# A convolution and whitening kernel: the first eight units' filters by a matmul of their own, and the store of all filters moved back in the queue

## The chip, the cores and the metric

The kernel runs on one core of a Trainium2 chip. The metric is the device time of one execution in microseconds (us), smaller is better; a kernel's time is the median of several runs.

## The reference

There are two layers. Layer 0 is a long convolution of each of 64 channels of x (4 images of 64 channels, 256 x 256) with a filter that is an outer product of two vectors of 256, which a small network makes from positions. Layer 1 whitens the result over the 64 channels. Cut to what matters:

```python
def _implicit_filter(z, w1, b1, w2, b2, w3, b3, wo, freq, t, deltas):
    h = jnp.sin(freq * (z @ w1 + b1))
    h = jnp.sin(freq * (h @ w2 + b2))
    h = jnp.sin(freq * (h @ w3 + b3))
    h = h @ wo
    decay = jnp.exp(-t * jnp.abs(deltas))
    return h * decay
...
k = jnp.einsum('ijk,imk->ijmk', hx, hy)[0]          # a rank-1 filter per channel
...                                                  # y = causal 2-D convolution of x with k, by FFT
out = y + x * bias[:, None, None]
...
x1_s = x1[:, ::STRIDE ** 2]                          # every 9th sample of each channel
mean1 = jnp.mean(x1_s, axis=-1, keepdims=True)
cov = x1_s @ x1_s.T / x1_s.shape[1] + EPS * jnp.eye(B, dtype=x.dtype)
deconv = _isqrt_newton_schulz(cov, N_ITER)
out = deconv @ (x1 - mean1)
```

## The kernel before

**Work.** A unit is one channel of two images, 128 units in all: 64 channels in a first sweep, the same 64 in a second. Since the filter is an outer product, a unit is two multiplications by Toeplitz matrices, one from the X filter (`make_v`, f = 0) and one from the Y filter (`make_y`, f = 1). TensorE does `make_v(q + 1)` and then `make_y(q)`, each of 16 matmuls (L731 to L734). Operands are split into a rounded part and a rest (hi and lo).

**Filters.** At the start TensorE, VectorE and ScalarE run the small network in three layers (L720, L553 to L556, L487). ScalarE's Exp (L484) makes the decay. VectorE multiplies the last product with it into `filt` (L561): 128 partitions, X filters of 64 channels and then Y filters. A Toeplitz matrix needs a filter shifted by one for each row. The filters are therefore stored to DRAM in 16 duplicates, and a load (a "hankel" load, L286 and L290) reads 64 rows of 320 values, each row one value later, from the 16 duplicates. ScalarE copies each half within SBUF to get the other 64 rows (`fill`, L453; L493 for unit 0), and writes the reversed matrices (`flip`, L462 and L463; L495 and L496 for unit 0). VectorE makes the lo part (`split_t`, L582; L605 for unit 0).

**Two stores.** The store of all filters (L328, four DMAs of 768 KB, 3.15 MB) is long. So a short one comes first: for the first AHEAD = 5 units, 5 rows in 16 duplicates for X from SyncE's queue and the same for Y from ScalarE's (`store_filters`, L249). The units 0 to 4 load from that (`first_dram`), the others from `g_dram`.

**Order.** Every engine's order is written by hand, with semaphores. SyncE issues all transfers but one, in one queue:

```python
store_filters(sp, 0)
for q in range(AHEAD):
    if q == H_SLOTS:
        load_x(AHEAD - 1)
    load_hankel(q)
for k in range(0, COPIES, COPIES // 4):
    sp.dma_start(copies_of(g_dram, k, ...), filt...).then_inc(filt_stored, 16)
for q in range(UNITS):
    if q > 0:
        load_x(q + 4)
    store_y(q - 1)
    if q == 0:
        sp.wait_ge(filt_stored, 16 * 4)
    load_hankel(q + 5)
    load_kept(q)
```

There are 5 slots for x, 3 for hankel loads and 3 for the reversed matrices, so `load_hankel(q)` waits until unit q - 3 has been flipped and split. Per unit ScalarE does `round_v(q)` (L479, L481), `round_x(q + 2)` (L472), `flip(q + 2)`, `fill(q + 3)`; VectorE does `split_v(q)` (L573), `finish_y(q - 1)` (L593, which writes y and waits for the store of the y before it in the same of two buffers), `split_t(q + 2)`, `sum_masked(q - 2)` (L601); POOL does `split_x(q + 2)` (L393) and `mask_y(q - 1)` (L428). Between the last layer and unit 0 TensorE runs 15 matmuls on zeros (`warm_up(15)`, L708), which are not used.

After the last unit come the covariance, the Newton-Schulz steps and 64 tiles of the whitened output. That part is not touched.

Of the kernel before, what the change touches and what calls it, by code (L numbers as in the profile page):

```python
# [6 lines left out]
F32 = mybir.dt.float32  # L7
F32R = mybir.dt.float32r
I32 = mybir.dt.int32
ALU = mybir.AluOpType  # L10
# [20 lines left out]
AHEAD = 5  # L31
# [37 lines left out]
def conv_whiten(nc, x, first, hidden, columns, bias, out):  # L69
    g_dram = nc.dram_tensor("filters", [COPIES, COPY_PITCH], F32, kind="Internal").ap()  # L70
    first_dram = nc.dram_tensor("first_filters", [COPIES, COPY_PITCH], F32, kind="Internal").ap()
    y_dram = nc.dram_tensor("convolved", [SWEEPS * P, ROWS * XW], F32, kind="Internal").ap()

    with ExitStack() as ctx:
# [57 lines left out]
        chan_i, chan, rate = sb("chan_i", [P, 1], I32), sb("chan", [P, 1]), sb("rate", [P, 1])  # L132


        arg, near_int, hid, pos_f, pos, decay = (kept[:, k * S:(k + 1) * S] for k in range(6))
        rest = kept[:, 14 * S + MASK_COLS:15 * S + MASK_COLS]
# [46 lines left out]
        first_stored = [sem(f"first_stored{f}") for f in range(2)]  # L183
# [72 lines left out]
        def _(sp):  # L256
# [16 lines left out]
            def load_hankel(q):  # L273
# [5 lines left out]
                wait(sp, t_lo_done, q - H_SLOTS + 1)  # L279
                for f in range(2):  # L280
                    at = (f * C + q % C) * GLEN
                    spread = [[COPY_PITCH + HALF // COPIES, COPIES], [1, HALF // COPIES], [1, HW]]
# [6 lines left out]
                    src = bass.AP(tensor=g_dram.tensor, offset=at, ap=spread)  # L289
                    sp.dma_start(h_own[k][f], src).then_inc(hankel_loaded[k], 16)  # L290
# [29 lines left out]


            store_filters(sp, 0)
            for q in range(AHEAD):
                if q == H_SLOTS:
                    load_x(AHEAD - 1)
                load_hankel(q)
            for k in range(0, COPIES, COPIES // 4):
                sp.dma_start(copies_of(g_dram, k, COPIES // 4, 0, 2 * C),  # L328
                             filt.unsqueeze(1).to_broadcast([P, COPIES // 4, GLEN])).then_inc(filt_stored, 16)
            for q in range(UNITS):  # L330
# [3 lines left out]
                if q == 0:  # L334
                    sp.wait_ge(filt_stored, 16 * 4)
# [42 lines left out]
        def _(pool):  # L378
# [8 lines left out]
            def split_x(q):  # L387
                if q >= UNITS:
# [6 lines left out]

            nc.gpsimd.memset(idle, 0.0).then_inc(idle_ready, 1)
            nc.gpsimd.memset(w_sb, 0.0).then_inc(w_zeroed, 1)
            nc.gpsimd.iota(pos_i, pattern=[[-1, S]], base=S - 1, channel_multiplier=0)
            chained(nc.gpsimd.iota(chan_i[:], pattern=[[0, 1]], base=0, channel_multiplier=1))
            nc.gpsimd.tensor_copy(pos, pos_i)  # L400
            nc.gpsimd.tensor_copy(chan[:], chan_i[:]).then_inc(pos_ready, 1)
            nc.gpsimd.memset(filt, 0.0).then_inc(filt_zeroed, 1)
            nc.gpsimd.memset(small[:], 0.0).then_inc(filt_zeroed, 1)
# [40 lines left out]
        def _(act):  # L444
# [10 lines left out]
            def flip(q):  # L455
# [3 lines left out]
                act.wait_ge(h_filled, 2 * (q + 1))  # L459
# [24 lines left out]
            nc.scalar.activation(decay, pos, ACT.Exp, scale=rate[:]).then_inc(decay_ready, 1)  # L484
# [3 lines left out]
            store_filters(act, 1)  # L488
# [398 lines left out]
```

## Time and profile before

| | |
|---|---|
| median of 3 runs | 920.75 us (919.14 to 922.94) |
| profiled execution | 922.17 us, of which the traced span is 920.4 us |
| busy in the span | PE 867.4, DVE 576.6, ACT 516.5, POOL 494.5 us |
| first matmul of unit 0 | 22.37 us |
| mean granted clock of TensorE | 0.99 of full speed |

Read it as follows: the span is the traced part of one execution; the time around it is 1.8 us. An engine's busy time says how near it is to be the bound, and the views by time say where it waits.

### The profile page before, as it was taken

What the parts mean: (1) busy time and instruction counts of PE and PEld (TensorE: products, weight loads), DVE (VectorE), ACT (ScalarE), POOL (GpSimd) and SP (SyncE); (2) the same over time, 40 slices, a digit from 0 to 9 for tenths busy, and PEclk for the clock granted to TensorE, in tenths of its full rate; (3) what the DMA queues carried; (4) which work ended last, traced back from release to release, by engine and by line L of the source; (5) the groups of instructions that cost most, each with busy time, mean ns of one, the idle gap of its engine ahead of it and who ended that gap; (6) DMA issues with size and microseconds to landing.
All of it is one profiled execution on the core that took longest, in us unless ns stands there. A gap on an engine that the chain in (4) does not pass through costs nothing.

```text
span 920.4 us, 16281 instructions
## 1 busy us (share of the span) xinstructions
PE 867.4 (94%) x6252; PEld 729.0 (79%) x6252; DVE 576.6 (63%) x630; ACT 516.5 (56%) x974; POOL 494.5 (54%) x279
## 2 busy tenths in 40 slices
PE   7989999999999999999999999998999999877773
PEld 5989999999999999999999999998544444323221
DVE  3488888878888867888888888885333333322221
ACT  3667777777777756777777777771233332222120
POOL 1488888888888876777777777772000000000000
PEclk9999999999999999999999999999999999999997
DMA  3788888888888885999999999987999999999998
GB/s 127 251 266 260 264 265 262 264 266 264 263 264 264 266 262 187 335 316 321 315 328 322 326 315 327 312 284 275 413 394 427 427 427 427 427 426 427 427 427 360
DMA packets 80899, 294.07 MB, mean 320 GB/s; under 512 B 11253, under 2 KB 29878, under 8 KB 66230
## 3 DMA queue, kind: packets, MB, share of 16 engines
q1 hardware_dynamic: 80737, 292.90, 88.5%
q8 instruction: 50, 0.82, 0.3%
q14 instruction: 27, 0.22, 0.1%
q10 hardware_dynamic: 85, 0.12, 0.0%
HBM read 155.37 MB, written 137.61 MB: 318 GB/s over the span
## 4 chain that ended last, share of the span: by engine, by line
PE 81%; DMA 13%; DVE 2%; SPq 1%; ACT 1%; issue 1%; POOL 0%; DVEq 0%; ACTq 0%; POOLq 0%
PE ps L734 24%; PE ps L853 15%; PE ps L731 13%; PE ps L732 13%; PE ps L733 13%; DMA arena<-convolved 11%; PE ps L773 2%; DMA filters<-arena 1%; DMA first_filters<-arena 1%; SPq L344 1%; PE ps L793 0%; PE ps L708 0%; DVE arena L699 0%; SPq L328 0%; PE ps L720 0%
## 5 line engine op out<-in xcount | busy, mean ns | idle before, releaser
L734 PE MATMUL ps<-arena 128*128 128x128 f32 x2048 | 394.2, 274 | 0.0
L731 PE MATMUL ps<-rounded 128*128 128x256 f32 x1024 | 374.0, 365 | 7.0 <-DVE rounded L605 3.0
L428 POOL TENSOR_TENSOR arena<-arena,mask 128x1024 f32<-128x1024 f32 x126 | 325.6, 2584 | 82.0 <-DVE arena L593 81.9
L734 PEld LDWEIGHTS ps<-arena 128*128 128x128 f32 x2048 | 316.6, 190 | 0.0
L733 PE MATMUL ps<-rounded 128*128 128x256 f32 x1024 | 289.1, 282 | 0.0
L732 PE MATMUL ps<-rounded 128*128 128x256 f32 x1024 | 288.4, 282 | 0.0
L853 PE MATMUL ps<-arena 128*128 128x512 f32 x488 | 216.0, 597 | 26.6 <-DMA arena<-convolved 26.5
L593 DVE SCALAR_TENSOR_TENSOR arena<-arena,bias_sb,ps 128x1024 f32<-128x1024 f32 x127 | 162.6, 1280 | 78.4 <-PE ps L734 75.1
L853 PEld LDWEIGHTS ps<-arena 128*128 128x128 f32 x488 | 90.7, 190 | 150.9 <-issue 105.0
L731 PEld LDWEIGHTS ps<-rounded 128*128 128x128 f32 x1024 | 196.9, 192 | 8.0 <-issue 6.6
L732 PEld LDWEIGHTS ps<-rounded 128*128 128x128 f32 x1024 | 197.5, 193 | 0.0
L733 PEld LDWEIGHTS ps<-rounded 128*128 128x128 f32 x1024 | 193.2, 189 | 0.0
L393 POOL TENSOR_TENSOR rounded<-arena,rounded 128x512 fp32r<-128x512 f32 x128 | 164.6, 1286 | 52.8 <-ACT rounded L472 52.8
L699 DVE TENSOR_SCALAR arena<-ps,small 128x1024 f32<-128x1024 f32 x64 | 82.1, 1283 | 171.6 <-PE ps L853 171.6
L525 ACT ACTIVATE arena<-ps,small 128x1024 f32<-128x1024 f32 x64 | 71.3, 1114 | 189.7 <-PE ps L853 189.7
L601 DVE TENSOR_REDUCE arena<-arena 128x116 f32<-128x1044 f32 x126 | 155.5, 1234 | 0.0
L573 DVE TENSOR_TENSOR rounded<-ps,rounded 128x512 fp32r<-128x512 f32 x128 | 88.5, 692 | 46.5 <-ACT rounded L481 46.5
L479 ACT COPY arena<-ps 128x512 f32<-128x512 f32 x128 | 75.0, 586 | 72.5 <-PE ps L734 72.5
L453 ACT COPY arena<-arena 64x256 f32<-64x256 f32 x254 | 102.9, 405 | 12.3 <-DMA arena<-filters 6.1
L462 ACT COPY arena<-arena 128x256 f32<-128x256 f32 x127 | 51.5, 405 | 77.9 <-PE ps L734 77.9
L582 DVE TENSOR_TENSOR rounded<-arena,rounded 128x512 fp32r<-128x512 f32 x127 | 88.4, 696 | 2.8 <-ACT rounded L463 2.8
L472 ACT CAST rounded<-arena 128x512 fp32r<-128x512 f32 x128 | 79.5, 621 | 6.2 <-DVE arena L561 1.9
(100 smaller groups left out, 295.4 us busy)
## 6 DMA issues: line engine op xcount, KB each, us to landing
arena<-x SPq DMA_DIRECT2D x128, 512.0 KB, 4.7
convolved<-arena SPq DMA_DIRECT2D x128, 512.0 KB, 5.7
out<-arena SPq DMA_DIRECT2D x64, 1024.0 KB, 13.4
arena<-convolved SPq DMA_DIRECT2D x47, 1024.0 KB, 18.6
arena<-filters SPq DMA_DIRECT2D x246, 80.0 KB, 4.4
arena<-convolved SPq DMA_DIRECT2D x28, 512.0 KB, 5.6
filters<-arena SPq DMA_DIRECT2D x4, 768.0 KB, 6.2
rounded<-convolved SPq DMA_DIRECT2D x3, 1024.0 KB, 8.9
```

Of the source, the lines that this page charges most:

```text
L393: nc.gpsimd.tensor_tensor(x_lo[k], row_block(q % X_SLOTS, 0), x_hi[k].bitcast(F32), ALU.subtract).then_inc(x_lo_done, 1)
L428: nc.gpsimd.tensor_tensor(masked_of(k, 0, PER), by_image(y_sb[k]), mask_of(q // C, 0, PER), ALU.mult).then_inc(masked_done, 1)
L453: nc.scalar.copy(h_copied[h][f], h_source[h][f]).then_inc(h_filled, 1)
L573: nc.vector.tensor_tensor(v_lo[k], ps_v[k][:, :, 0:S], v_hi[k].bitcast(F32), ALU.subtract).then_inc(v_lo_done, 1)
L582: nc.vector.tensor_tensor(t_lo[k], hankel[h][:, :, ::-1], t_hi[k].bitcast(F32), ALU.subtract).then_inc(t_lo_done, 1)
L593: nc.vector.scalar_tensor_tensor(y_sb[k], x_sb[q % X_SLOTS], bias_sb[:, q % C:q % C + 1], ps_y[k].rearrange("p a n -> p (a n)"), ALU.mult, ...
L601: nc.vector.tensor_reduce(z_of(q % C), grouped(q % 2, 0, BLOCKS), AX_X, ALU.add).then_inc(z_done, 1)
L731: mm(wide, hi[:, b, cols], t_hi[k][:, f, :], start=True, stop=False)
L732: mm(wide, hi[:, b, cols], t_lo[k][:, f, :], start=False, stop=False)
L733: mm(wide, lo[:, b, cols], t_hi[k][:, f, :], start=False, stop=False)
L734: last = mm(o[:, b, m * S + P:(m + 1) * S], block1[:, b, cols], t_f32[k][:, f, :], start=False, stop=True)
L853: last = mm(ps[:, bank(t, u) + r, :], dmat, places[k][:, w:w + IMG], start=True, stop=True)
```

## The change

Six things are changed together.

1. The first units are now eight (AHEAD = 8). POOL makes a weight matrix `first_w` in which the last layer's column of each of eight channels, X and Y, stands eight times: 2 x 8 x 8 = 128 columns. One more matmul in the last layer (L741) puts each filter in eight partitions, VectorE multiplies it with its own decay (L575), and one DMA of 128 rows (L327), each partition to a row of its own, stores them. ScalarE's store is gone. The factor 1/(2S) on the X filters, which was an instruction of its own (L547), becomes `share`, a factor per partition in the last multiply.
2. The loads for units 0 to 7 read from these eight duplicates. For unit 0 they read all 128 rows, and the two half copies (L493) and their waits are gone.
3. In SyncE's queue unit 3's load comes before x(4), two quarters of the store of all filters come next, then unit 4's load, then the other two quarters; `load_hankel(5)` is issued without a wait for that store. Unit 8's load is the first with the wait `filt_stored`.
4. On ScalarE `fill(q + 2)` stands ahead of `round_x(q + 2)` and `flip(q + 2)`; before, it was one unit earlier, at the end of the step.
5. The channel numbers for the decay are made first on POOL, with a semaphore `chan_ready`, and VectorE computes two decay rates from them with more, small operations.
6. ScalarE computes two Exp instead of one and waits for `pos_ready` ahead of them.

The diff, cut:

```diff
-AHEAD = 5
+AHEAD, FIRST_COPIES = 8, 8
+FIRST_PITCH = 4096 + 128
...
-        def store_filters(eng, f):
-            eng.wait_ge(filt_ready, 1)
-            eng.dma_start(copies_of(first_dram, 0, COPIES, f * C, AHEAD),
-                          filt[f * C:f * C + AHEAD, :].unsqueeze(1).to_broadcast([AHEAD, COPIES, GLEN])
-                          ).then_inc(first_stored[f], 16)
...
+                if q == AHEAD:
+                    sp.wait_ge(filt_stored, 16 * 4)
                 for f in range(2):
                     if q < AHEAD:
-                        sp.wait_ge(first_stored[f], 16)
-                        src = bass.AP(tensor=first_dram.tensor, offset=at, ap=spread)
-                        sp.dma_start(h_own[k][f], src
+                        rows, cols = (HALF, HW) if q else (P, S)
+                        n = FIRST_COPIES
+                        src = bass.AP(tensor=first_dram.tensor, offset=(f * AHEAD + q) * n * FIRST_PITCH,
+                                      ap=[[FIRST_PITCH + rows // n, n], [1, rows // n], [1, cols]])
+                        sp.dma_start(h_own[k][f] if q else hankel[0][:, f, :], src
...
-            store_filters(sp, 0)
-            for q in range(AHEAD):
-                if q == H_SLOTS:
-                    load_x(AHEAD - 1)
+            sp.wait_ge(first_made, 1)
+            sp.dma_start(first_dram[:, 0:GLEN], first_filt).then_inc(first_stored, 16)
+            sp.wait_ge(first_stored, 16)
+            for q in range(H_SLOTS + 1):
                 load_hankel(q)
+            load_x(4)
+            sp.wait_ge(filt_ready, 1)
             for k in range(0, COPIES, COPIES // 4):
                 sp.dma_start(copies_of(g_dram, k, COPIES // 4, 0, 2 * C),
                              filt.unsqueeze(1).to_broadcast([P, COPIES // 4, GLEN])).then_inc(filt_stored, 16)
+                if k == COPIES // 4:
+                    load_hankel(4)
             for q in range(UNITS):
                 if q > 0:
                     load_x(q + 4)
                 store_y(q - 1)
-                if q == 0:
-                    sp.wait_ge(filt_stored, 16 * 4)
                 load_hankel(q + 5)
...
+            pool.wait_ge(hidden_loaded, 16 * 2)
+            of_first = w_sb[:, 2, :].rearrange("p (f c) -> p f c", f=2)[:, :, 0:AHEAD].unsqueeze(3)
+            nc.gpsimd.tensor_copy(first_w.rearrange("p (f c k) -> p f c k", f=2, c=AHEAD),
+                                  of_first.to_broadcast([P, 2, AHEAD, FIRST_COPIES])).then_inc(first_w_ready, 1)
...
             act.wait_ge(rate_ready, 1)
-            nc.scalar.activation(decay, pos, ACT.Exp, scale=rate[:]).then_inc(decay_ready, 1)
+            act.wait_ge(pos_ready, 1)
+            nc.scalar.activation(first_decay, pos, ACT.Exp, scale=rate[:, 1:2]).then_inc(decay_ready, 1)
+            nc.scalar.activation(decay, pos, ACT.Exp, scale=rate[:, 0:1]).then_inc(decay_ready, 1)
...
-            store_filters(act, 1)
...
-                nc.scalar.copy(h_copied[0][f], h_source[0][f]).then_inc(h_filled, 1)
-                act.wait_ge(h_filled, f + 1)
...
-            fill(2)
             for q in range(UNITS):
                 round_v(q)
+                fill(q + 2)
                 round_x(q + 2)
                 flip(q + 2)
-                fill(q + 3)
...
-            nc.vector.tensor_tensor(filt[:, 0:S], ps[:, 0, 0:S], decay, ALU.mult).then_inc(filt_ready, 1)
+            nc.vector.scalar_tensor_tensor(first_filt[:, 0:S], ps[:, 1, 0:S], share[:], first_decay, ALU.mult, ALU.mult
+                                           ).then_inc(first_made, 1)
+            dve.wait_ge(f_mm, 5)
+            nc.vector.scalar_tensor_tensor(filt[:, 0:S], ps[:, 0, 0:S], share[:], decay, ALU.mult, ALU.mult
+                                           ).then_inc(filt_ready, 1)
...
+                if layer == 2:
+                    pe.wait_ge(first_w_ready, 1)
+                    mm(ps[:, 1, 0:S], first_w, hid, start=True, stop=True).then_inc(f_mm, 1)
```

SyncE's queue from the first filters' store on, before (`first_filters` is `first_dram`, `filters` is `g_dram`, `arena` holds the slots in SBUF, `convolved` receives y):

```order
L286 DMA arena<-first_filters 64x1x320 [waits first_stored0]
L286 DMA arena<-first_filters 64x1x320 [waits first_stored1]
L271 DMA arena<-x 128x1024
L286 DMA arena<-first_filters 64x1x320 [waits first_stored0,t_lo_done,flipped]
L286 DMA arena<-first_filters 64x1x320 [waits first_stored1]
L286 DMA arena<-first_filters 64x1x320 [waits first_stored0,t_lo_done,flipped]
L286 DMA arena<-first_filters 64x1x320 [waits first_stored1]
L328 DMA filters<-arena 128x4x384 x4
L290 DMA arena<-filters 64x1x320 [waits t_lo_done,flipped,filt_stored]
L290 DMA arena<-filters 64x1x320
L271 DMA arena<-x 128x1024 [waits y_done]
```

and after, from the same place:

```order
L289 DMA arena<-first_filters 64x1x320 x4
L289 DMA arena<-first_filters 64x1x320 [waits t_lo_done,flipped]
L289 DMA arena<-first_filters 64x1x320
L271 DMA arena<-x 128x1024
L334 DMA filters<-arena 128x4x384 [waits filt_ready]
L334 DMA filters<-arena 128x4x384
L289 DMA arena<-first_filters 64x1x320 [waits t_lo_done,flipped]
L289 DMA arena<-first_filters 64x1x320
L334 DMA filters<-arena 128x4x384 x2
L289 DMA arena<-first_filters 64x1x320 [waits t_lo_done,flipped]
L289 DMA arena<-first_filters 64x1x320
L271 DMA arena<-x 128x1024 [waits y_done]
```

Unit 3's loads, with their waits for unit 0's flip and split, now stand ahead of x(4), the pair for unit 4 stands inside the store, and the pair for unit 5, behind it, no longer waits for `filt_stored`.

ScalarE's step for unit 1, before (L479 and L481 are `round_v`, L472 `round_x`, L462 and L463 `flip`, L453 `fill`):

```order
L479 COPY arena<-ps 128x512 [waits v_mm]
L481 CAST rounded<-ps 128x512
L472 CAST rounded<-arena 128x512 [waits v_mm,x_loaded3]
L462 COPY arena<-arena 128x256 [waits y_mm,h_filled]
L463 CAST rounded<-arena 128x512
L453 COPY arena<-arena 64x256 [waits hankel_loaded1]
L453 COPY arena<-arena 64x256
L479 COPY arena<-ps 128x512 [waits y_mm,v_mm]
```

and after (L489 and L491, L482, L472 and L473, L463 in the same order):

```order
L489 COPY arena<-ps 128x512 [waits v_mm]
L491 CAST rounded<-ps 128x512
L463 COPY arena<-arena 64x256 [waits hankel_loaded0]
L463 COPY arena<-arena 64x256
L482 CAST rounded<-arena 128x512 [waits v_mm,x_loaded3]
L472 COPY arena<-arena 128x256 [waits y_mm,h_filled]
L473 CAST rounded<-arena 128x512
```

The two copies of `fill`, then for unit 4 and now for unit 3, have moved from behind the flip to directly behind `round_v`.

ScalarE's first rows, before:

```order
L484 ACT_TABLE_LOAD
L484 ACTIVATE arena<-arena,rate 128x256 [waits rate_ready]
L487 ACT_TABLE_LOAD
L487 ACTIVATE arena<-arena 128x256 [waits f_dve] x3
```

and after:

```order
L495 ACT_TABLE_LOAD [waits pos_ready]
L495 ACTIVATE arena<-arena,rate 128x256 [waits rate_ready]
L496 ACTIVATE arena<-arena,rate 128x256
L499 ACT_TABLE_LOAD
L499 ACTIVATE arena<-arena 128x256 [waits f_dve] x3
```

The load of the first activation table, which stood ahead of every wait, now carries the wait for `pos_ready`.

## Rows read from the trace of the kernel before

**Rows 1.** The page, part 1: busy us (share of the span) and instructions.

```profile
PE 867.4 (94%) x6252; PEld 729.0 (79%) x6252; DVE 576.6 (63%) x630; ACT 516.5 (56%) x974; POOL 494.5 (54%) x279
```

**Rows 2.** Busy time by stretch: stretch and length, engines, PEclk, DMA share, GB/s.

```profile
49.40:53.00 3.60, 3.60 (x18) 3.60 (x19) 3.60 (x4) 2.35 (x6) 3.60 (x3) 0.53 0.90 270
60.00:70.00 10.00, 10.00 (x89) 10.00 (x87) 7.63 (x9) 7.09 (x15) 8.78 (x6) 1.00 0.86 274
```

**Rows 3.** Timeline of ScalarE: start, length, line, operation [idle before <-releaser].

```profile
20.93 0.40 ACT L493 COPY arena<-arena 64x256 f32<-64x256 f32 x1 [6.30 <-DMA arena<-first_filters]
...
23.05 0.83 ACT L453 COPY arena<-arena 64x256 f32<-64x256 f32 x2
...
24.73 0.61 ACT L463 CAST rounded<-arena 128x512 fp32r<-128x512 f32 x1
...
41.56 0.83 ACT L453 COPY arena<-arena 64x256 f32<-64x256 f32 x2 [4.43 <-DMA arena<-filters]
...
67.41 0.59 ACT L479 COPY arena<-ps 128x512 f32<-128x512 f32 x1 [0.48 <-PE ps L734]
...
72.05 0.59 ACT L479 COPY arena<-ps 128x512 f32<-128x512 f32 x1 [0.48 <-PE ps L734]
```

**Rows 4.** Timeline, rows of TensorE: the starts after a stop, and the warm-up.

```profile
12.68 6.64 PE L708 MATMUL ps<-arena 128*128 128x256 f32 x30
...
22.37 0.55 PE L731 MATMUL ps<-rounded 128*128 128x256 f32 x1 [3.05 <-DVE rounded L605]
...
26.65 0.36 PE L731 MATMUL ps<-rounded 128*128 128x256 f32 x1 [0.27 <-DVE rounded L582]
...
44.14 0.39 PE L731 MATMUL ps<-rounded 128*128 128x256 f32 x1 [1.10 <-DVE rounded L573]
...
49.34 0.45 PE L731 MATMUL ps<-rounded 128*128 128x256 f32 x1 [2.62 <-issue]
```

**Rows 5.** Waits of SyncE's own queue, 0 to 60 us: total, times, longest.

```profile
SPq L290 <- DMA filters<-arena: 6.1, 1, 6.1
```

**Rows 6.** Timeline of SyncE's queue: issue and time to issue.

```profile
13.44 0.30 SPq L249 DMA_DIRECT2D first_filters<-arena  x1
18.64 3.75 SPq L286 DMA_DIRECT2D arena<-first_filters  x6
...
27.77 4.72 SPq L328 DMA_DIRECT2D filters<-arena  x4
38.64 1.16 SPq L290 DMA_DIRECT2D arena<-filters  x2
```

**Rows 7.** Timeline of VectorE: split_t while POOL splits, and alone.

```profile
25.38 1.13 DVE L582 TENSOR_TENSOR rounded<-arena,rounded 128x512 fp32r<-128x512 f32 x1 [2.10 <-ACT rounded L463]
...
66.39 0.69 DVE L582 TENSOR_TENSOR rounded<-arena,rounded 128x512 fp32r<-128x512 f32 x1
```

**Rows 8.** Timeline of ScalarE before the filters.

```profile
0.73 1.28 ACT L484 ACT_TABLE_LOAD   x1 [0.73 <-PEq L878]
...
3.06 0.51 ACT L484 ACTIVATE arena<-arena,rate 128x256 f32<-128x256 f32 x1 [1.05 <-DVE rate L543]
...
5.80 0.42 ACT L487 ACTIVATE arena<-arena 128x256 f32<-128x256 f32 x1 [0.93 <-DVE arena L556]
```

**Rows 9.** Timeline of POOL: positions, and split_x and mask_y of a steady unit.

```profile
1.94 0.40 POOL L400 CAST arena<-arena 128x256 f32<-128x256 int32 x1
...
69.28 1.30 POOL L393 TENSOR_TENSOR rounded<-arena,rounded 128x512 fp32r<-128x512 f32 x1
71.19 2.78 POOL L428 TENSOR_TENSOR arena<-arena,mask 128x1024 f32<-128x1024 f32 x1 [0.61 <-DVE arena L593]
```

**Rows 10.** Busy time by stretch: DMA share and GB/s at the end.

```profile
14.50:15.00 0.50, 0.50 (x4) 0.45 (x3) 0.47 (x2) 0.13 (x1) 0.29 (x1) 1.00 0.31 55
20.00:20.60 0.60, 0.00 (x0) 0.00 (x0) 0.00 (x0) 0.00 (x0) 0.00 (x0) 1.00 0.49 130
29.00:37.00 8.00, 8.00 (x72) 8.00 (x72) 5.17 (x6) 6.62 (x14) 5.83 (x4) 1.00 1.01 362
```

More of the change, by code:

```diff
@@ L70, in conv_whiten @@
     g_dram = nc.dram_tensor("filters", [COPIES, COPY_PITCH], F32, kind="Internal").ap()
-    first_dram = nc.dram_tensor("first_filters", [COPIES, COPY_PITCH], F32, kind="Internal").ap()
+    first_dram = nc.dram_tensor("first_filters", [P, FIRST_PITCH], F32, kind="Internal").ap()
     y_dram = nc.dram_tensor("convolved", [SWEEPS * P, ROWS * XW], F32, kind="Internal").ap()
@@ L131, in conv_whiten @@
         col = sb("col", [P, 5])
-        chan_i, chan, rate = sb("chan_i", [P, 1], I32), sb("chan", [P, 1]), sb("rate", [P, 1])
+        chan_i, chan, rate = sb("chan_i", [P, 2], I32), sb("chan", [P, 2]), sb("rate", [P, 2])
+        share = sb("share", [P, 1])
         arg, near_int, hid, pos_f, pos, decay = (kept[:, k * S:(k + 1) * S] for k in range(6))
+        first_decay, first_filt = kept[:, 17 * S:18 * S], kept[:, 18 * S:18 * S + GLEN]
+        first_w = kept[:, 20 * S:20 * S + P]
         rest = kept[:, 14 * S + MASK_COLS:15 * S + MASK_COLS]
@@ L182, in conv_whiten @@
         bias_loaded, w_zeroed, idle_ready = sem("bias_loaded"), sem("w_zeroed"), sem("idle_ready")
-        first_stored = [sem(f"first_stored{f}") for f in range(2)]
+        first_w_ready, first_made, first_stored = sem("first_w_ready"), sem("first_made"), sem("first_stored")
+        chan_ready = sem("chan_ready")
         first_hankel = [sem(f"first_hankel{f}") for f in range(2)]
@@ L394, in split_x @@
                                         ALU.subtract).then_inc(x_lo_done, 1)
+            nc.gpsimd.iota(chan_i[:], pattern=[[0, 2]], base=0, channel_multiplier=1).then_inc(chan_ready, 1)
             nc.gpsimd.memset(idle, 0.0).then_inc(idle_ready, 1)
             nc.gpsimd.memset(w_sb, 0.0).then_inc(w_zeroed, 1)
[L398 to L401, printed above, removed]
+            chained(nc.gpsimd.iota(pos_i, pattern=[[-1, S]], base=S - 1, channel_multiplier=0))
+            nc.gpsimd.tensor_copy(pos, pos_i).then_inc(pos_ready, 1)
             nc.gpsimd.memset(filt, 0.0).then_inc(filt_zeroed, 1)
+            nc.gpsimd.memset(first_filt, 0.0).then_inc(filt_zeroed, 1)
             nc.gpsimd.memset(small[:], 0.0).then_inc(filt_zeroed, 1)
@@ L537, in chained @@
                 dve.wait_ge(step_sem, n_step[0])
-            dve.wait_ge(pos_ready, 1)
+            nc.vector.memset(share[0:C, :], 1.0 / (2 * S))
+            chained(nc.vector.memset(share[C:P, :], 1.0))
+            dve.wait_ge(chan_ready, 1)
             step = (MAX_DEC - MIN_DEC) / (C - 1)
-            chained(nc.vector.tensor_scalar(rate[0:C, :], chan[0:C, :], -step, -MIN_DEC, ALU.mult, ALU.add))
-            chained(nc.vector.tensor_scalar(rate[C:P, :], chan[C:P, :], -step, C * step - MIN_DEC, ALU.mult, ALU.add))
+            chained(nc.vector.tensor_scalar(chan_i[:, 0:1], chan_i[:, 0:1], C - 1, None, ALU.bitwise_and))
+            chained(nc.vector.tensor_scalar(chan_i[:, 1:2], chan_i[:, 1:2], 3, AHEAD - 1,
+                                            ALU.logical_shift_right, ALU.bitwise_and))
+            chained(nc.vector.tensor_copy(chan[:], chan_i[:]))
+            chained(nc.vector.tensor_scalar(rate[:], chan[:], -step, -MIN_DEC, ALU.mult, ALU.add))
             nc.vector.tensor_scalar(rate[:], rate[:], 1.0 / (S - 1), None, ALU.mult).then_inc(rate_ready, 1)
```

16 lines of the change are left out of this document (7 added, 9 removed).

## Prediction

> **What bounds the kernel now.** I read the page first, then the same execution from its start. TensorE is busy 867.4 of 920.4 us [rows 1], so the time to be had is where it waits or runs slowly. In the long first stage it waits for nothing: in the stretch from 60 to 70 us it is busy throughout at full clock [rows 2]. The marks that I use for its progress are the starts of ScalarE's copy of the V of a unit (L479), which comes right after TensorE ends that unit's `make_v`. Units 8 and 9 have it at 67.41 and 72.05 us [rows 3]: 4.64 us per unit, two halves (`make_v` and `make_y`) of 2.32 us. Counted back from unit 8 at 4.64 us each, unit 1 would have had its mark at 67.41 - 7 x 4.64 = 34.93 us. TensorE really began `make_v(1)` at 26.65 us [rows 4] and so ended it at 28.97, a mark of about 29.05. Between units 1 and 8 the kernel therefore loses 34.93 - 29.05 = **5.88 us**.
>
> Where: the waits of SyncE's own queue name the filters' DMA, 6.1 us at once [rows 5]. SyncE issues the big store of all filters from 27.77 us and can issue unit 5's load (L290) only at 38.64 [rows 6]; the next x load and y store stand behind it in its queue. ScalarE stops 4.43 us in `fill(5)`, until 41.56 [rows 3], with `round_v(3)`, which TensorE waits for, behind it. TensorE stops 1.10 us before 44.14 and 2.62 us before 49.34 [rows 4], and after the second stop its granted clock is 0.53 for 3.6 us, that is, nearly all of it at the lower level, 1.2 GHz [rows 2].
>
> The same at the start: the store of the first filters is issued at 13.44 and its readers at 18.64 [rows 6], 5.2 us; ScalarE starts at 20.93 on what they brought [rows 3], VectorE follows, and TensorE starts `make_v(0)` at 22.37 after 3.05 us without work [rows 4].
>
> **The change, part by part.** *Before the filters.* ScalarE's first table load takes 1.28 us and ran from 0.73 us, under other work [rows 8]. By the order it now stands behind `pos_ready`. POOL's conversion of the positions ended near 2.34 [rows 9]; the `iota` put before it costs about 0.15, one conversion less is behind it: pos_ready at 2.5. Then 1.28 for the table, two Exp of 0.51 [rows 8] (0.95 together if they overlap a little), and 1.28 for the Sin table: 6.0 us, where Sin started at 5.80 [rows 8]. Cost +0.2. VectorE's seven small operations, on at most two columns, end before this and cost nothing: their cover is the table load. None of their kind is in the rows; even at 0.5 us each, the time of Exp over 256 columns, they would end near 4.4, 0.6 after the table. One more fp32 matmul in the last layer is 0.44 us on TensorE, by the 15 warm-up matmuls in 6.64 us [rows 4], but it comes first and its product is taken first, so the path sees none of it; the multiply with a factor more may take 0.1 longer. The store is issued at 13.44 + 0.25 = 13.7. The warm-up then ends at about 20.0 (19.32 before).
>
> *The first store.* The old one held the DMA engines at a share of 0.31 [rows 10]: 5 source rows, 5 of 16 engines (0.31), each with 16 rows of 1536 bytes from each of two queues. Its 5.2 us less some 0.8 to the first byte are 4.4, or 137 ns a row. The new one is 128 rows in one DMA, 8 an engine if all 16 share. In bulk, the big store moved such rows at 362 GB/s, 68 ns a row and engine [rows 10]. So 8 x 68 to 8 x 137 ns = 0.55 to 1.1 us, plus 0.6 to 0.8 before the first byte and 0.2 after: 1.4 to 2.1 us; I take 2.0, near the upper bound, because short transfers here never reach the bulk rate. The readers are issued at 15.7.
>
> *The first loads.* An old load of 80 KB landed 2.3 us after issue, of which its rows took a share of 0.49 of 0.6 us, 0.3 us of each engine's time [rows 10]: with 4 rows an engine and the packet that signals, 60 to 75 ns a row. (2.3 is 20.93 less the issue at 18.64.) The new source has 8 duplicates as its outer step where the old had 16, and unit 0's loads have 128 rows in place of 64. If only 8 engines carry them (a case with no row here but the 5 engines of the old store), a load for unit 0 is 16 rows an engine, about 60 ns each for 1 KB, 0.95 us, and one for unit 1 8 rows, 0.55 us. They queue: data flow from 17.05 (15.7 + 1.35), the first is usable at 18.5, the second at 19.4, unit 1's pair at 20.4. If 16 engines carry them, unit 1's pair is usable at 20.0. Forecast: 20.4.
>
> A rule speaks against this part. The row shows an old store with 5 outer rows at a share of 0.31, and nothing on 8. The Trainium skill, "DMA: Bandwidth & Descriptors", section "Why a DMA increments its semaphore by 16 and not by 1", says that a DMA runs on the largest number of engines up to 16 that divides the slowest dimension of both sides. By it the old store had 5 (the trace agrees, 0.31), the new store has 16, and the new loads have 8. With 16 the sum would be 0.4 us better.
>
> *ScalarE at the start.* The two half copies (0.40 each) for unit 0 are gone. From unit 1's landing at 20.4: `fill(1)`, `round_x(1)` and `flip(1)` took 2.3 us from 23.05 to 25.34 [rows 3], VectorE's split 1.13 [rows 7]: 23.85. `make_v(0)` needs only the first load and the warm-up: 20.0 to 22.3 at full clock. `make_v(1)` starts at 24.0 in place of 26.65: **gain 2.65 us**, with 1.6 us of stop before it, which is nearer to the stop of 1.10 us than to that of 2.62: the matmul behind the first took 0.39 us, behind the second 0.45, and behind the 3.05 us at the start 0.55 [rows 4]. So I charge no slow clock.
>
> *The store of all filters.* Unit 8's load is the first to wait for it. SyncE issues units 0 to 2's loads until 19.5, unit 3's after unit 0's split (20.7), x(4), two quarters of the store, unit 4's load (after unit 1's split, 23.9), the other two, unit 5's load. What moves behind 20.7 until it all has landed: 3.15 MB of filters, x(4) and three pairs of loads, 4.2 MB, at 362 GB/s 11.5 us, so near 33. `fill(4)` is wanted at the mark of unit 2, 31.2, and its load stands behind only half of the store (28). `fill(5)` and x(5), issued after `finish_y(0)` at 30.2, are wanted at 36.8 and 37.6; x(5) lands by 35.6. The store of y(0) lands near 37 and `finish_y(2)` wants it at 38.1; what waits behind that on VectorE is `split_t(5)`, which TensorE needs at 42.7. Nothing is late by these numbers, by 1 to 5 us. **Gain 5.88 us.**
>
> *The steady order.* `fill(q + 2)` now stands ahead of `round_x(q + 2)`, 0.83 us more ahead of POOL's split. That split ran at 69.28, and would run at 70.0 to 71.3; POOL's masking began at 71.19 because of VectorE [rows 9], and so begins 0.1 later. `make_v(10)` wants both splits at 74.2. Zero, hidden by 2.3 us.
>
> Sum: 2.65 + 5.88 = 8.5. The profiled execution took 922.17 us and its span is 920.4; it would give 913.7. It is 1.4 us above the median of the three runs, 920.75, which would give 912.2. I count from halfway, 921.5: **913.0**.
>
> **Rivals.** *The clock falls at unit 1.* If the first loads take 80 ns a row on 8 engines, unit 1's pair comes at 21.3, and the stop before `make_v(1)` is 2.6 us, as the one that was followed by 3.6 us at 0.53. Price 0.9 + 1.7 us (half of 3.6, nearly): gain 5.9, 915.6. For it speaks that the old store kept to 5 engines with 5 rows, against it that old rows took no more than 75 ns. The Trainium skill's rule above, 8 engines, is this rival's condition. *The stall comes back in part.* From 20 to 37 us the queue must carry 5.3 MB, 310 GB/s with little spare, and on 8 engines the loads weigh double. If x(5) and y(0) come 3 us after their wants, TensorE loses some 2 us and perhaps the clock's 1.7: gain 4.8, 916.7. *The start stays as it was* (store or loads land as late as before, ScalarE's first piece again at 20.9): then only the two half copies, 0.83 us, are saved: gain 6.7, 914.8. *The other side:* POOL or VectorE becomes the bound of all 126 steady units. A VectorE split that meets a POOL split takes 1.13 in place of 0.69 [rows 7], and POOL's later split now touches it. VectorE is busy 7.63 of 10 us there [rows 2], 3.5 us of a unit's 4.64, 4.0 with that; it decides only above 4.64. Were it 4.75, the loss is 126 x 0.11 = 14 us, less 8.5: 927. I see 0.6 us missing for it.
>
> **How the numbers follow.** Forecast 0.50; slow clock 0.17; stall in part 0.16; start as before 0.12; the other side 0.05. A measurement tells about 0.5%, 4.6 us, from none: all of the first and second and most of the others lie beyond, or 0.85 faster, 0.11 same, 0.04 slower. The best case (16 engines, store 1.4 us) gains 9.5, 912.0, and the runs shown lie within 2 us of their median. The range is 909.8 to 917.0; it leaves out the slow side and the worst of the partial stall.
>
> **What would show it.** Right: readers of the first filters issued 2 us after the store; TensorE starting near 20.0 with no stop; unit 8's mark near 58.9 (67.41 - 8.5); no wait for the filters' DMA; unit periods of 4.64. Wrong: a first mark of unit 1 near 29, a clock near 0.5 about 24 to 28 us, a stop around 37 to 45 us, or unit periods above 4.64.

## The result, and the profile after

The changed kernel takes 916.41 us (median of 10 runs, 913.96 to 919.59), the one before 921.71 us (10 runs, 919.14 to 925.1). The ratio is 0.9942, with a 95% interval of 0.9925 to 0.9959: faster by 5.3 us, between 3.8 and 6.9. The forecast was 8.5 us and 913.0. The profiled execution took 914.88 us with a span of 913.1, which is 7.3 us less than the span before. Of the later executions of the changed kernel one took 4971 us; it is counted as slow and stands in no ratio.

The page of the changed kernel, part 1 and two groups of part 5 (TensorE's wait before the first matmul of a group, VectorE's `split_t`, whose mean was 696 ns before):

```profile
PE 864.6 (95%) x6254; PEld 726.7 (80%) x6254; DVE 600.3 (66%) x634; ACT 504.4 (55%) x973; POOL 502.1 (55%) x280
...
L753 PE MATMUL ps<-rounded 128*128 128x256 f32 x1024 | 372.8, 364 | 2.1 <-DVE rounded L600 2.1
...
L600 DVE TENSOR_TENSOR rounded<-arena,rounded 128x512 fp32r<-128x512 f32 x127 | 112.6, 887 | 4.3 <-ACT rounded L473 4.3
```

TensorE waits 2.1 us in all before the groups. Against that stand the stops of 3.05, 1.10 and 2.62 us of [rows 4]. VectorE is busy 24 us longer, nearly all of it in `split_t`.

The timeline of SyncE's queue in the changed kernel, to be held against [rows 6]:

```profile
13.68 0.33 SPq L327 DMA_DIRECT2D first_filters<-arena  x1
15.55 6.51 SPq L289 DMA_DIRECT2D arena<-first_filters  x8
...
22.60 0.98 SPq L334 DMA_DIRECT2D filters<-arena  x2
24.30 1.76 SPq L289 DMA_DIRECT2D arena<-first_filters  x2
26.10 2.33 SPq L334 DMA_DIRECT2D filters<-arena  x2
28.54 2.41 SPq L289 DMA_DIRECT2D arena<-first_filters  x2
```

The readers of the first filters are issued 1.87 us after the store in place of 5.2. The store of all filters begins 5.2 us earlier, and unit 5's load follows it at 28.54, where it was issued at 38.64.

ScalarE at the start and at the marks of units 1, 2, 8 and 9 (start, length, line, and in brackets the idle time before), to be held against [rows 3]:

```profile
18.42 0.40 ACT L504 CAST rounded<-arena 128x256 fp32r<-128x256 f32 x1 [5.65 <-DMA arena<-first_filters]
...
19.92 0.41 ACT L504 CAST rounded<-arena 128x256 fp32r<-128x256 f32 x1 [0.90 <-DMA arena<-first_filters]
...
20.78 0.84 ACT L463 COPY arena<-arena 64x256 f32<-64x256 f32 x2 [0.25 <-DMA arena<-first_filters]
...
26.96 0.59 ACT L489 COPY arena<-ps 128x512 f32<-128x512 f32 x1 [0.59 <-PE ps L756]
...
31.60 0.59 ACT L489 COPY arena<-ps 128x512 f32<-128x512 f32 x1 [1.23 <-PE ps L756]
...
59.44 0.59 ACT L489 COPY arena<-ps 128x512 f32<-128x512 f32 x1 [1.23 <-PE ps L756]
...
64.09 0.59 ACT L489 COPY arena<-ps 128x512 f32<-128x512 f32 x1 [1.24 <-PE ps L756]
```

Unit 8's mark is at 59.44, and 26.96 + 7 x 4.64 = 59.44: not a tenth of a microsecond is lost between units 1 and 8. Against 67.41 that is 7.97 us.

TensorE has one stop left between units 0 and 8, before `make_v(1)`:

```profile
24.37 0.36 PE L753 MATMUL ps<-rounded 128*128 128x256 f32 x1 [2.13 <-DVE rounded L600]
```

Two stretches of the changed kernel in the form of [rows 2] (the last three columns are the granted clock, the DMA share and GB/s). In the first the store of 128 rows moves, in the second the loads of units 0 to 2:

```profile
14.40:15.20 0.80, 0.80 (x5) 0.72 (x4) 0.73 (x3) 0.00 (x0) 0.57 (x3) 1.00 0.68 246
17.00:21.20 4.20, 4.20 (x27) 3.86 (x26) 0.85 (x2) 1.62 (x5) 0.00 (x0) 1.00 0.44 139
```

### The profile page after: what moved, and what is told of

Its sections match the earlier page's. It is cut to its first block, busy times and chain, and to the rows that moved or that the text cites. A ratio compares the mean times of both kernels' runs of the same rounds, so it can differ in the third digit from the quotient of the medians.

```text
span 913.1 us, 16292 instructions
## 1 busy us (share of the span) xinstructions
PE 864.6 (95%) x6254; PEld 726.7 (80%) x6254; DVE 600.3 (66%) x634; ACT 504.4 (55%) x973; POOL 502.1 (55%) x280
## 4 chain that ended last, share of the span: by engine, by line
PE 83%; DMA 12%; DVE 2%; SPq 1%; issue 0%; ACT 0%; POOL 0%; DVEq 0%; POOLq 0%
PE ps L756 25%; PE ps L875 15%; PE ps L753 13%; PE ps L754 13%; PE ps L755 13%; DMA arena<-convolved 11%; PE ps L795 2%; PE ps L726 1%; DVE arena L717 1%; PE ps L815 0%; SPq L350 0%; DMA arena<-first_filters 0%; PE ps L852 0%; DMA first_filters<-arena 0%; SPq L289 0%
## 5 line engine op out<-in xcount | busy, mean ns | idle before, releaser
L438 POOL TENSOR_TENSOR arena<-arena,mask 128x1024 f32<-128x1024 f32 x126 | 333.9, 2650 | 3.1 <-DVE arena L611 2.9
L489 ACT COPY arena<-ps 128x512 f32<-128x512 f32 x128 | 75.1, 587 | 163.1 <-PE ps L756 163.1
L600 DVE TENSOR_TENSOR rounded<-arena,rounded 128x512 fp32r<-128x512 f32 x127 | 112.6, 887 | 4.3 <-ACT rounded L473 4.3
L463 ACT COPY arena<-arena 64x256 f32<-64x256 f32 x254 | 103.0, 406 | 6.5 <-DMA arena<-first_filters 0.2
L482 ACT CAST rounded<-arena 128x512 fp32r<-128x512 f32 x128 | 79.4, 620 | 3.6 <-DMA arena<-x 0.5
L473 ACT CAST rounded<-arena 128x512 fp32r<-128x512 f32 x127 | 78.3, 617 | 0.0
```

Of the source, the lines that this page charges most:

```text
L438: nc.gpsimd.tensor_tensor(masked_of(k, 0, PER), by_image(y_sb[k]), mask_of(q // C, 0, PER), ALU.mult).then_inc(masked_done, 1)
L463: nc.scalar.copy(h_copied[h][f], h_source[h][f]).then_inc(h_filled, 1)
L600: nc.vector.tensor_tensor(t_lo[k], hankel[h][:, :, ::-1], t_hi[k].bitcast(F32), ALU.subtract).then_inc(t_lo_done, 1)
```

## The experiments

Each kernel was timed against the kernel before in three or five rounds, in three groups. Each group ran on a chip of its own beside the kernel before, so only ratios are compared between groups. The unit marks in the text are the starts of ScalarE's copy of V, as in the prediction. "Period" is the distance of two marks in undisturbed units. All marks, periods and clocks are those of one traced execution of each kernel; the ratio is of all its executions.

| kernel | ratio to before, 95% interval | mark of unit 8, us | period before and after unit 66, us |
|---|---|---|---|
| before, first trace | | 67.41 | 4.64, 4.61 |
| before again | 0.9998 (0.998 to 1.0015) | 65.62 | 4.61, 4.61 |
| changed, first trace | 0.9942 (0.9925 to 0.9959) | 59.44 | 4.64, 4.61 |
| changed, second | 0.9956 (0.9937 to 0.9976) | 59.70 | 4.64, 4.64 |
| changed, third | 0.9947 (0.9928 to 0.9967) | 60.64 | 4.61, 4.64 |
| changed, old tensor size | 0.994 (0.9917 to 0.9963) | 60.89 | 4.64, 4.64 |
| SyncE's order alone | 0.997 (0.995 to 0.999) | 61.88 | 4.64, 4.61 |
| changed, wait at unit 5 | 0.9967 (0.9951 to 0.9984) | 63.92 | 4.64, 4.64 |
| changed, 16 outer steps | 0.9931 (0.9904 to 0.9958) | 59.14 | 4.61, 4.64 |
| changed, old fill order | 0.9918 (0.9899 to 0.9937) | 59.32 | 4.61, 4.61 |
| 16 steps and old fill order | 0.9908 (0.989 to 0.9927) | 58.46 | 4.61, 4.64 |
| the same again | 0.992 (0.9895 to 0.9944) | 58.52 | 4.64, 4.64 |
| 16 steps, x before fill | 0.9938 (0.9915 to 0.996) | 58.85 | 4.64, 4.61 |
| before with the new fill order | 1.002 (0.9999 to 1.0041) | 65.80 | 4.64, 4.61 |

**The changed kernel again.** The question was why the medians give 5.3 us where the two spans give 7.3.

> The changed kernel unaltered. Theory A (the early steps are worth what its first trace shows, 8.0 us at unit 8's mark, and what the median gives less is the later part of the run that varies): unit 8's mark again at 59.2 to 59.7 us, unit 127's near 617.4, and the difference of the span to the first trace, whatever it is, behind that. Rival B (the first trace is a lucky one, a stall comes back in most executions): the mark is at 60.5 or later with a stop of TensorE between units 1 and 8.

The mark of unit 8 is at 59.70. Rival B is out for this execution; TensorE's one stop is 1.75 us, and it waits for nothing between units 1 and 8. The span is nevertheless 917.3, 4.2 us more: 1.6 between the marks of units 8 and 127 (559.47 us against 557.91), because the period stays 4.64 to the end, and 2.1 from the first whitening tile to the end (269.6 against 267.5), a part in which TensorE waits for DMA 27.0 us in all in the first trace. Over all fourteen traces that last part is 266.7 to 269.9 us, whatever the kernel.

**SyncE's order alone.** The kernel before, with

```diff
-AHEAD = 5
+AHEAD = 8
...
+                if q == AHEAD:
+                    sp.wait_ge(filt_stored, 16 * 4)
...
-            for q in range(AHEAD):
-                if q == H_SLOTS:
-                    load_x(AHEAD - 1)
+            for q in range(H_SLOTS + 1):
                 load_hankel(q)
+            load_x(4)
...
+                if k == COPIES // 4:
+                    load_hankel(4)
...
-                if q == 0:
-                    sp.wait_ge(filt_stored, 16 * 4)
```

> The kernel before with eight first units and SyncE's new order, the old first store, the old unit 0 and the old order on ScalarE. If the part between units 1 and 8 is SyncE's wait alone: unit 1's mark near 29.1, unit 8's at 61.5, 5.9 us earlier than before, time 0.994 to 0.996 of before. Rival (ScalarE's new order is needed, since fill(5) stood ahead of round_v(3)): fill(5) waits again and the mark is 62.5 or later.

The mark is at 61.88, the start as late as before. ScalarE does wait in `fill`, 1.80 and 1.14 us:

```profile
34.51 0.83 ACT L454 COPY arena<-arena 64x256 f32<-64x256 f32 x2 [1.80 <-DMA arena<-first_filters]
...
38.92 0.83 ACT L454 COPY arena<-arena 64x256 f32<-64x256 f32 x2 [1.14 <-DMA arena<-first_filters]
```

but no stop of TensorE follows between units 1 and 8. So SyncE's order alone brings the part between units 1 and 8, and ScalarE's new order was not needed for it. By the ratio, though, this is 2.8 us (0.9 to 4.6), not the 5.5 us between this mark and that of the first trace of before; against the second trace of before (65.62) the mark is 3.7 us earlier.

**The wait at unit 5 again**, in the changed kernel:

```diff
-                if q == AHEAD:
-                    sp.wait_ge(filt_stored, 16 * 4)
...
+                if q == 0:
+                    sp.wait_ge(filt_stored, 16 * 4)
                 load_hankel(q + 5)
```

> The changed kernel with the wait for the store of all filters ahead of unit 5's load again. If that wait is what cost 5.9 us: the mark of unit 8 goes back towards 65. If the earlier store and ScalarE's order are enough: the store is issued 5 us earlier than before and has landed at 34 to 35, unit 5's load at 37, wanted at 37.4, and the mark is at 59.5 to 61.

The mark goes back to 63.92, against 59.44 to 60.64. The view of SyncE's waits and three rows of the timeline (ScalarE, ScalarE, TensorE):

```profile
SPq L287 <- DMA filters<-arena: 7.1, 1, 7.1
```

```profile
38.86 0.83 ACT L463 COPY arena<-arena 64x256 f32<-64x256 f32 x2 [1.83 <-DMA arena<-first_filters]
41.25 0.62 ACT L482 CAST rounded<-arena 128x512 fp32r<-128x512 f32 x1 [1.55 <-DMA arena<-x]
...
45.86 0.35 PE L753 MATMUL ps<-rounded 128*128 128x256 f32 x1 [3.02 <-issue]
```

The store has landed by 35.34, 0.3 us behind the time expected, but unit 5's load is only the first of the transfers behind it: x(5), issued at 36.60, lands when it is needed long since. TensorE stops 3.02 us before `make_v(5)`, and the clock is 0.66 from 46 to 48 us and 0.50 from 48 to 50. What ends last before that stop is neither unit 5's load nor x(5) but VectorE, which waits 6.12 us for the store of y(0) and has `split_t(5)` behind it, done at 45.76:

```profile
43.88 1.28 DVE L611 SCALAR_TENSOR_TENSOR arena<-arena,bias_sb,ps 128x1024 f32<-128x1024 f32 x1 [6.12 <-DMA convolved<-arena]
45.08 0.68 DVE L600 TENSOR_TENSOR rounded<-arena,rounded 128x512 fp32r<-128x512 f32 x1
```

The stop of 2.62 us before 49.34 in the kernel before has the same cause. The store of y(0) stands behind the wait in SyncE's queue there too, and `split_t(5)` is done at 49.24:

```profile
47.36 1.28 DVE L593 SCALAR_TENSOR_TENSOR arena<-arena,bias_sb,ps 128x1024 f32<-128x1024 f32 x1 [3.28 <-DMA convolved<-arena]
48.56 0.68 DVE L582 TENSOR_TENSOR rounded<-arena,rounded 128x512 fp32r<-128x512 f32 x1
```

In the trace an earlier store does not replace the removed wait. In the time it is hard to see: the ratio is 0.0011 above that of the changed kernel in the same group, and the intervals overlap.

**Sixteen outer steps** in the loads of units 0 to 7:

```diff
-                                      ap=[[FIRST_PITCH + rows // n, n], [1, rows // n], [1, cols]])
+                                      ap=[[rows // 16, 16], [FIRST_PITCH + 1, rows // 16], [1, cols]])
```

> The changed kernel, the loads of units 0 to 7 with 16 outer steps of 8 or 4 rows from as many duplicates, the same values. If the number of engines sets their time (share 0.4 to 0.5 in the trace): share near 0.9 while a load runs, unit 1's pair usable at 20.0 in place of 20.8, the stop of 2.13 us before make_v(1) falls to 1.2, unit 8's mark 0.9 earlier, 58.5. If the rows' own latency or the issue of 0.6 us a load sets it: no change.

The share while loads run is 0.67 to 0.78, where it was 0.44:

```profile
18.00:19.00 1.00, 1.00 (x7) 0.87 (x6) 0.00 (x0) 0.05 (x1) 0.00 (x0) 1.00 0.78 238
19.00:20.00 1.00, 1.00 (x6) 0.90 (x5) 0.54 (x2) 1.00 (x4) 0.00 (x0) 1.00 0.67 150
```

ScalarE gets the second load 3.21 us after the first issue (19.46 - 16.25), where it was 4.37 (19.92 - 15.55), and unit 1's pair after 4.42 in place of 5.23. The stop before `make_v(1)` falls from 2.13 to 1.32 us. In this execution the filters themselves were 0.7 us later, so the mark is only 0.3 earlier; its sisters below have 58.46 to 58.85. So the walk over the source set the time of the loads, and by the share it did so through the number of engines at work.

**The old size of the DRAM tensor**, so that what lies behind it is not moved (the store's target is written out to match, with the same pitch):

```diff
-    first_dram = nc.dram_tensor("first_filters", [P, FIRST_PITCH], F32, kind="Internal").ap()
+    first_dram = nc.dram_tensor("first_filters", [COPIES, COPY_PITCH], F32, kind="Internal").ap()
...
-            sp.dma_start(first_dram[:, 0:GLEN], first_filt).then_inc(first_stored, 16)
+            sp.dma_start(bass.AP(tensor=first_dram.tensor, offset=0, ap=[[FIRST_PITCH, P], [1, GLEN]]), first_filt).then_inc(first_stored, 16)
```

> The changed kernel with the DRAM tensor of the first filters declared as large as before (3.2 MB in place of 2.2), so that the y tensor behind it lies where it lay. Theory A (what the median gives less than the trace is variation between executions): ratio 0.993 to 0.996, the part from the first whitening tile to the end 267 to 269.5 us as in the other traces. Rival C (the shifted y tensor makes the DMA-bound part slower): that part 267.2 or less and the ratio at 0.992.

Ratio 0.994, last part 268.4 us, between the changed kernel's 267.5 and 269.9: nothing speaks for rival C, though the interval (0.9917 to 0.9963) holds its 0.992 too. The start brought something else: `make_v(1)` begins at 24.26 after a stop of 2.03 us, and the clock is 0.50 from 26 to 28 us; its unit 8 is at 60.89.

**The old fill order** in the changed kernel (`fill(2)` ahead of the loop, `fill(q + 3)` behind `flip(q + 2)`):

```diff
+            fill(2)
             for q in range(UNITS):
                 round_v(q)
-                fill(q + 2)
                 round_x(q + 2)
                 flip(q + 2)
+                fill(q + 3)
```

> The changed kernel with fill(q + 3) at the end of ScalarE's step as before. Sum's view (the new order is worth nothing either way in the steady units): unit 8's mark at 59.5 unless a late load shows, VectorE's split_t back from 0.88 to 0.69 us, ratio as the changed kernel, 0.994 to 0.996. Rival D (the new order costs, as TensorE's period after unit 66 was 4.64 us in three of four traces with it and 4.61 in both without): period 4.61 after unit 66 and 1.5 us less, ratio 0.992 to 0.994. If the new order was needed early: fill waits for a load and the mark is 60.5 or later.

Mark at 59.32 with waits in `fill` of 0.41, 1.20 and 0.43 us that cost TensorE nothing. `split_t` is back:

```profile
L601 DVE TENSOR_TENSOR rounded<-arena,rounded 128x512 fp32r<-128x512 f32 x127 | 87.8, 692 | 3.9 <-ACT rounded L473 3.9
```

The ratio is 0.9918, below all four of the changed kernel's. The period is 4.61 in both stretches.

**The kernel before again.**

> The kernel before unaltered, against itself. Theory A: unit 8's mark at 67.2 to 67.7, ratio 0.998 to 1.002; the periods of 4.64 and 4.61 us and the last part may come out otherwise than in the first trace. Rival D: 4.61 again after unit 66.

The mark is at 65.62, outside what was expected, and the clock explains most of it. The stop before `make_v(5)` is 2.14 us here and no slow clock follows it, where 2.62 us in [rows 4] were followed by one:

```profile
49.21 0.36 PE L731 MATMUL ps<-rounded 128*128 128x256 f32 x1 [2.14 <-issue]
```

The slow clock at the start is in both. So the first trace of before, from which the sum was made, holds one slow clock more than this one.

**Sixteen steps and the old fill order together**, in two groups:

> The changed kernel with loads of 16 outer steps and with fill(q + 3) at the end of the step. Theory A: unit 8's mark at 58.5 to 59.2, ratio 0.992 to 0.994. Rival D: a further 1.5 us less than the kernel with 16 outer steps alone, period 4.61 after unit 66.

> The kernel with loads of 16 outer steps and the old fill order, a second time. Rival D: ratio 0.990 to 0.992, at least one stretch at 4.61 us. Theory A (run to run variation alone): ratio anywhere in 0.990 to 0.995, and not below the changed kernel's in this call by more than 0.001.

Marks at 58.46 and 58.52, as expected; ratios 0.9908 and 0.992. The first has a period of 4.61 in one stretch, the second in none, which rival D did not expect. But the second's traced execution, 916.89 us, was the slowest of its six (the fastest took 911.21), so its two long stretches don't speak for the five others and say nothing against D. This is the fastest version measured, some 7 to 8 us below the kernel before. In its two groups it stands 0.0032 and 0.0027 below the changed kernel (with the old tensor size in the first, unaltered in the second).

**The new fill order in the kernel before**, the reverse edit:

> The kernel before with only ScalarE's order changed (fill(q + 2) ahead of round_x(q + 2)). It takes fill(5) from ahead of round_v(3), so the early stall may shrink. Rival D (the new order makes TensorE's period more often 4.64 than 4.61 us, 1.7 us for each of the two stretches of some 60 units): VectorE's split_t at 0.88 us, period 4.64 in at least one stretch, and whatever the early part gains is lost again: ratio 0.997 to 1.002. If the order is free in the steady units and early on: 0.994 to 0.998 with unit 8's mark 2 us or more earlier.

1.002, interval 0.9999 to 1.0041, with `split_t` at 881 ns and a period of 4.64 in one stretch. Its mark, 65.80, lies between the two of before. The stop of 1.10 us is gone, but `fill(5)` still waits 1.80 us and x(5) is 2.06 us late. VectorE waits 5.42 us for the store of y(0), until 45.75, and TensorE stops 2.28 us before `make_v(5)` as a result. Alone the order gives nothing and may cost.

**x before fill**, with 16 outer steps (`round_v`, `round_x`, `fill`, `flip`):

> The changed kernel with loads of 16 outer steps and ScalarE's order round_v, round_x(q + 2), fill(q + 2), flip(q + 2). POOL's split then runs at its old time, apart from VectorE's split_t. If the meeting of the two splits is what makes the long period more frequent: split_t 0.69 us, period 4.61, ratio 0.990 to 0.992 like the old order. If it is the late flip: period 4.64 at least once and 0.993.

`split_t` is at 701 ns, so in the steady units the two splits no longer meet; the ratio is 0.9938 and the period 4.64 in one stretch, the numbers expected of the late flip. Two things keep this from being an answer. The interval (0.9915 to 0.996) holds the old order's ratios too. And this order has a loss of its own right behind the covariance, at unit 68, where units follow each other faster. The marks of units 68 and 69 in the kernel before, in the changed kernel and here:

```profile
353.89 0.57 ACT L479 COPY arena<-ps 128x512 f32<-128x512 f32 x1
357.50 0.59 ACT L479 COPY arena<-ps 128x512 f32<-128x512 f32 x1 [0.22 <-PE ps L734]
```

```profile
345.92 0.58 ACT L489 COPY arena<-ps 128x512 f32<-128x512 f32 x1
349.78 0.59 ACT L489 COPY arena<-ps 128x512 f32<-128x512 f32 x1 [0.47 <-PE ps L756]
```

```profile
345.33 0.58 ACT L489 COPY arena<-ps 128x512 f32<-128x512 f32 x1
350.30 0.59 ACT L489 COPY arena<-ps 128x512 f32<-128x512 f32 x1 [1.58 <-PE ps L756]
```

That is 3.61, 3.86 and 4.97 us. `split_t(69)`, which TensorE needs next, took 0.74 us in the first, 1.06 in the second and 2.17 in the third. Without the 1.1 us that it loses there against the changed kernel, its ratio would be near 0.9926 (an estimate from this one trace).

**The changed kernel, third trace.**

> The changed kernel unaltered, a third trace. Rival D: ratio 0.994 to 0.996, at least one stretch at 4.64 us. The clock may fall at make_v(1), as in one of four traces with this start so far: then unit 8's mark is near 61, else 59.2 to 59.7.

The clock fell. The same stretch in the first trace and in this one:

```profile
24.40:28.00 3.60, 3.60 (x31) 3.60 (x32) 1.50 (x2) 2.96 (x7) 1.29 (x1) 1.00 0.96 338
```

```profile
24.40:28.00 3.60, 3.60 (x23) 3.60 (x23) 1.32 (x2) 2.16 (x5) 1.28 (x1) 0.67 1.03 392
```

In these 3.6 us 23 matmuls are recorded against 31, and unit 8's mark is at 60.64. The stop before was 1.97 us, shorter than the first trace's 2.13.

## Why the prediction was right, and where its sizes were off

*Direction and mechanism held.* The time, 916.41, is in the range of 909.8 to 917.0, but near its upper end. The gain is 5.3 us of the forecast 8.5.

*Before the filters.* Forecast +0.25 us, store issued at 13.7; it was 13.68. Sin starts at 5.97 (6.0 forecast), because the table load waits until 2.44. Right to the tenth in this trace; in two of the ten traces with this start (the second of the changed kernel and 16 outer steps) the store is issued only at 14.3 and 14.4.

*The first store.* Forecast 2.0 us, measured 1.87. Its rows take a share of 0.68 over 0.8 us, that is, 0.54 us an engine or 68 ns for each of 8 rows. I had left the bulk rate out as out of reach for a short transfer; it was reached. What is not rows took 1.33 us, where I had 0.8 to 1.0. So the 2.0 us came close by two errors that cancel, which is luck.

*The first loads.* The condition that decided was the 8 engines: the share is 0.44 in 4.2 us (8 of 16 would give at most 0.50), and with 16 outer steps 0.67 to 0.78. Under the Trainium skill's rule ("DMA: Bandwidth & Descriptors", "Why a DMA increments its semaphore by 16 and not by 1") the loads have 8 engines; the traces agree. 6 loads are 64 rows on each of 8 engines (2 x 16 and 4 x 8) and took 4.2 us, 66 ns a row where I had 60 and 69; the mean was fair. The mis-sized term was the second load of 1 KB rows, usable 1.5 us after the first, where I had 0.9. Unit 1's pair was usable at 20.78, not 20.4, and `make_v(1)` began at 24.37, not 24.0. The start gave 26.65 - 24.37 = 2.3 us by TensorE's own rows, or 2.1 by the marks, in place of 2.65. The start was not timed as a kernel of its own.

*The slow clock.* The rival "the clock falls at unit 1" is not a case of the kernel but of the execution. Of six traces that start as the changed kernel does, with stops of 1.75 to 2.22 us, two show it, and there it costs 1.6 us up to unit 8 (from the start of `make_v(1)` to unit 8's mark 36.63 us with the old tensor size, against 35.07 in the first trace, at the same period). I had decided by the nearer row, 1.10 us, as if the length of the stop told it. The step failed more on the side of before: its first trace had a clock that fell twice, and the second trace only once. Unit 8's mark is at 66.5 us in the mean of the two traces of before and at 59.9 in the mean of three of the changed kernel: 6.6 us, where the first pair says 8.0 and the sum said 8.5.

*The store of all filters.* The mechanism held: nothing is lost between units 1 and 8 of the changed kernel, and with the wait put back unit 8 is 3.3 to 4.5 us later. The size did not hold: the 5.88 us were those of one execution. The same reckoning on the second trace of before, where `make_v(1)` starts at 27.18 and unit 8's mark is at 65.62, gives 3.8 us. In the time, SyncE's order alone is worth 2.8 us (0.9 to 4.6), and putting the wait back costs 0.0011 in its group, or 0.0019 against the mean of the changed kernel's three, 1.0 to 1.8 us. Together with the steady order, below, this term accounts for most of the way from 8.5 to 5.3.

My times for the transfers behind the store were also 3 us too early:

```profile
38.80 0.62 ACT L482 CAST rounded<-arena 128x512 fp32r<-128x512 f32 x1 [0.54 <-DMA arena<-x]
39.91 1.28 DVE L611 SCALAR_TENSOR_TENSOR arena<-arena,bias_sb,ps 128x1024 f32<-128x1024 f32 x1 [1.86 <-DMA convolved<-arena]
```

x(5), forecast for 35.6, comes at 38.8 and is 0.5 us late; the store of y(0), forecast near 37, is awaited until 39.9 by `finish_y(2)`, 1.9 us late. Part of it is that the transfers did not start moving at 20.7: x(4), the first large one, was issued at 22.11. "Nothing is late" was wrong, then; what saved the forecast is that `split_t(5)` behind `finish_y(2)` was done at 41.79 and TensorE needed it only near 42.9. That is the path by which the old queue stopped TensorE for 2.62 us: about 1.1 us were to spare on it now.

*The steady order.* Forecast zero; this is the second mis-sized term. Three comparisons point the same way: the old order is lower by 0.0030 in the changed kernel (0.9918 against the mean of its three, 0.9948), by 0.0017 with 16 steps (0.9931 against the mean of 0.9908 and 0.992), and in the kernel before the new order is higher by 0.002. Their mean, 0.0022, is 2.1 us. Each one alone is within its intervals or at their edge. As a rough account, 6.6 - 2.1 = 4.5 us, against 5.3 (3.8 to 6.9) measured.

A quarter of a microsecond of it is in every trace: from unit 68's mark to unit 69's the new order takes 3.86 to 3.88 us and the old one 3.61 to 3.65, as in the lines shown with "x before fill". Between the marks of units 8 and 127, traces with one long and one short stretch take 557.9 us with the new order and 557.7 with the old. More of it may be the choice of TensorE's period told below (long in 10 of 14 stretches with the new order, in 5 of 12 with the old), but such counts also come by chance. The x before fill run does not decide it, as told there. The cause of the rest of the 2 us stays open; that the order isn't needed for the early gain is shown.

*The other rivals.* No VectorE or POOL bound: VectorE is busy 8.47 of 10 us there, 3.9 of 4.64, near the 4.0 worked out. "The stall comes back in part" came true for the two transfers, though not for TensorE. "The start stays as it was" did not happen.

## What to carry to other kernels

SyncE's queue, blocked for 6.1 us on one long store, delayed everything behind it, and the cost is not that of the first transfer alone: in the kernel before and with the wait put back, TensorE's longest stop between units 1 and 8 came by the store of y(0), two transfers further back, which VectorE awaited with work for TensorE behind it. Follow every transfer behind the wait to the engine that needs it; move the wait to where the data is first used, not only the store earlier. Count the outer steps of a source as well as those of the destination: going from 16 to 8 duplicates was harmless for the data and cost 0.8 us on the critical start, which a different walk through the same duplicates gave back. A sum made from one trace inherits that trace's accidents: the 5.88 us were 3.8 in the next trace. When the term is a few microseconds, take a second trace of the kernel before. And leave out an edit (here ScalarE's order) that the gain doesn't need.

## What the runs showed of the hardware that I had not expected

TensorE's steady period has two values at a granted clock of 1.00. Every trace has either 4.64 or 4.61 us a unit in each of its two long stretches, and where the two differ the change comes at unit 66, where the covariance interrupts the pattern. Two traces of the same changed kernel, ScalarE's marks at equal places of the second stretch, first trace:

```profile
497.41 0.59 ACT L489 COPY arena<-ps 128x512 f32<-128x512 f32 x1 [1.20 <-PE ps L756]
502.02 0.59 ACT L489 COPY arena<-ps 128x512 f32<-128x512 f32 x1 [1.21 <-PE ps L756]
```

and second trace:

```profile
498.54 0.59 ACT L489 COPY arena<-ps 128x512 f32<-128x512 f32 x1 [1.24 <-PE ps L756]
503.17 0.59 ACT L489 COPY arena<-ps 128x512 f32<-128x512 f32 x1 [1.23 <-PE ps L756]
```

0.027 us a unit is 1.6 us over a stretch. What sets it wasn't found.

The clock after a stop is not told by the stop's length. After stops of 2.03 and 1.97 us it fell to the lower level, after 2.13, 2.14 and 2.22 it did not; it fell after 2.28, 2.62, 3.02 (twice), 3.05 and 3.33 us, and did not after one of 3.07 us at the start of the kernel before with the new fill order. After the shorter ones, 0.84 to 1.93 us, no trace shows it. These are the stops between the warm-up and unit 8.
